# Ring items one by one and behind the maxima: a new order within the slots of an attention loop

## The reference, cut to what matters

```python
x = x + ln(attn(ln(x)))      # attn: qkv projection, 16 heads of 16, softmax, projection, z + out
x = x + ln(ffn(ln(x)))       # ffn: shared gated hidden layer of 128, and one of 8 experts for every second token
scores = einsum('bhqd,bhkd->bhqk', q, k) / 4
att = softmax(scores)
out = einsum('bhal,bhlv->bhav', att, v)
```

## Time and profile before

| | us |
|---|---|
| median of 3 runs | 984.24 (984.19 to 984.42) |
| the profiled execution | 983.9 |
| its span, first to last instruction | 982.1 |
| TensorE busy | 882.3 (90%) |
| VectorE busy | 792.7 (81%) |
| ScalarE busy | 663.7 (68%) |
| GpSimd busy | 314.5 (32%) |
| VectorE in row maxima (L1331), 1024 of them | 633.9, and 110.3 idle before them |
| ScalarE in exponentials (L873), 512 of them | 539.1, and 85.2 idle before them |

### The profile page before, as it was taken

How to read it: one execution, slowest core, us unless ns; L and a number is a source line. 1 busy time by engine, 2 the same in 40 slices (tenths; PEclk the granted TensorE clock), 3 DMA queues, 4 the chain that set the end, 5 groups by cost and what they waited for, 6 DMA issues and landing times. The chain is left out here.

```text
span 982.1 us, 14337 instructions
## 1 busy us (share of the span) xinstructions
PE 882.3 (90%) x5188; PEld 319.8 (33%) x5188; DVE 792.7 (81%) x1568; ACT 663.7 (68%) x728; POOL 314.5 (32%) x450
## 2 busy tenths in 40 slices
PE   6879999999999999999999999999989989757985
PEld 3312322222243233322332242322322313136863
DVE  4598879898979878899888879889799788265765
ACT  5128778787877787878877868788677768901110
POOL 4041010005424414139443423255243232822113
PEclk9769999999999999999999999999999989988998
DMA  5631010310320203101411022004310001240001
GB/s 143 105 45 39 16 53 16 73 41 10 90 61 13 93 12 70 38 13 55 89 61 56 12 39 59 23 7 105 91 56 14 11 13 31 85 172 23 1 1 64
DMA packets 52375, 49.08 MB, mean 50 GB/s; under 512 B 17504, under 2 KB 43696, under 8 KB 51920
## 3 DMA queue, kind: packets, MB, share of 16 engines
q1 hardware_dynamic: 51680, 46.91, 19.4%
q0 software_dynamic: 384, 1.05, 0.3%
q10 hardware_dynamic: 240, 0.20, 0.2%
HBM read 18.06 MB, written 9.17 MB: 28 GB/s over the span
## 5 line engine op out<-in xcount | busy, mean ns | idle before, releaser
L1331 DVE TENSOR_REDUCE mx<-ring 128x1 f32<-128x512 f32 x1024 | 633.9, 680 | 110.3 <-PE ring L1038 109.6
L873 ACT ACTIVATE prob<-sc,unscale 128x1024 f32<-128x1024 f32 x512 | 539.1, 1113 | 85.2 <-PE sc L1056 83.9
L1038 PE MATMUL ring<-kp,qp 48*128 48x512 f16 x1024 | 299.4, 395 | 43.5 <-DVE mx L1331 22.5
L1070 PE MATMUL obank<-prob,vaug 128*32 128x512 f32 x2048 | 276.1, 612 | 0.7 <-ACT prob L873 0.6
L1038 PEld LDWEIGHTS ring<-kp,qp 48*128 48x128 f16 x1024 | 74.1, 93 | 361.4 <-DVE mx L1331 301.3
L1056 PE MATMUL sc<-qp,kp 64*128 64x512 f16 x1024 | 167.9, 381 | 14.0 <-ACT prob L873 13.3
L644 POOL TENSOR_TENSOR parts<-qkf,parts 128x1024 f16<-128x1024 f32 x14 | 29.9, 2134 | 209.6 <-ACT parts L803 209.6
L1056 PEld LDWEIGHTS sc<-qp,kp 64*128 64x128 f16 x1024 | 50.4, 95 | 92.3 <-ACT prob L873 83.9
L631 POOL TENSOR_TENSOR hid<-hid,b 128x512 f32<-128x512 f32 x24 | 30.2, 1270 | 110.9 <-ACT hid L827 110.9
L639 POOL TENSOR_TENSOR yA<-yA,sums 128x512 f32<-128x512 f32 x15 | 19.0, 1269 | 131.1 <-DMA sums<-reciprocal_scratch 131.1
L1070 PEld LDWEIGHTS obank<-prob,vaug 128*32 128x32 f32 x2048 | 40.5, 108 | 61.5 <-issue 58.4
(11 more groups left out here) (221 smaller groups left out, 749.2 us busy)
## 6 DMA issues: line engine op xcount, KB each, us to landing
x_sb<-x SPq DMA_DIRECT2D x7, 1024.0 KB, 6.0
kp<-parts SPq DMA_DIRECT2D x48, 128.0 KB, 4.4
qp<-parts SPq DMA_DIRECT2D x93, 64.0 KB, 5.5
out<-hid SPq DMA_DIRECT2D x4, 1024.0 KB, 5.3
yA<-oT SPq DMA_DIRECT2D x124, 32.0 KB
sums<-reciprocal_scratch SPq DMA_DIRECT2D x31, 128.0 KB
x_scratch<-x SPq DMA_DIRECT2D x3, 1024.0 KB, 4.5
qp<-mp SPq DMA_DIRECT2D x128, 2.0 KB
```

Of the source, the lines that this page charges most:

```text
L873: nc.scalar.activation(prob[:, e % 2, 2 * a:2 * a + 2, :].rearrange("p g n -> p (g n)"), sbuf2[a][:, :], ACT.Exp, scale=unscale[:, 0:1]).t ...
L1038: nc.tensor.matmul(dst[:, :], qp[rows, qh, h, qt * P:(qt + 1) * P], kp[rows, h, kh * HALF:(kh + 1) * HALF], start=True, stop=True).then_in ...
L1070: ins = nc.tensor.matmul(obank[i * VW:(i + 1) * VW, :], vaug[:, b % 2, kt, c0:c0 + VW], prob[:, v % 2, i, :], start=(kt == 0), stop=(kt == ...
L1331: nc.vector.tensor_reduce(mx[:, u % 2, n:n + 1], src[:, :], AX.X, ALU.max).then_inc(rv_free, 1)
```

## The change

Within a slot TensorE now makes: maximum products 0 and 1, the value product of step e - 2, maximum products 2 and 3, the items, the scores of step e. ScalarE copies obank at the start of the slot after, ahead of the items; VectorE takes the four maxima first, then the casts, then the statistics. Items that stood in pairs get a slot each, and statistics are split and moved beside them. Slots of GpSimd's and SP's steps are moved to fit. The number of slots grows by one. No instruction is added or removed but that the statistics are taken in other portions. The diff:

```diff
--- before.py
+++ after.py
@@ -37,31 +37,32 @@
 SL = HU * NT
 NS = B * SL
 LEAD = 12
-SLOTS = NS + LEAD + 3
+SLOTS = NS + LEAD + 4
 
 
 
 QK_LEAD = (4, 5, 6, 7)
-QK_AT = (2, 2, 4, 4)
-Z_AT = ((18, 18, 20, 20), (9, 9, 17, 17))
-V_AT = (25, 25, 49, 49)
-P_AT = (19, 19, 21, 21)
-QK_NEXT_AT = (33, 33, 35, 35)
-X_AT = (41, 41, 42, 42)
-H_AT = (44, 44, 47, 47)
-U_AT = (57, 57)
-W_AT = (59, 59, 61, 61)
+QK_AT = (1, 2, 4, 5)
+Z_AT = ((17, 19, 21, 23), (9, 11, 13, 15))
+V_AT = (26, 28, 51, 53)
+P_AT = (17, 19, 22, 24)
+QK_NEXT_AT = (33, 35, 37, 39)
+X_AT = (41, 42, 43, 44)
+H_AT = (45, 46, 48, 49)
+U_AT = (57, 58)
+W_AT = (59, 60, 61, 62)
 
 MT_AT = (2, 9, 17, 25, 33, 41, 49, 57)
 
 
-Z_STATS = ((9, 10), (2, 2))
-Y_STATS = (21, 21, 25, 25)
+Z_STATS = ((9, 10), (1, 2))
+Y_STATS = (19, 22, 24, 26)
 X_STATS = (33, 35)
-F_AT = ((4, 4), (0, 1))
-
-
-D_AT = (43, 51, 14, 19)
+U_STATS = (51, 53)
+F_AT = ((4, 5), (0, 1))
+
+
+D_AT = (44, 52, 15, 21)
 
 ROWS = 16 * (1 + GH)
 
@@ -90,7 +91,7 @@
         add(1 <= w < B, W_AT, *(("w", w - 1, i) for i in range(4)))
         mt = [("mt", t // 8 - 1)] if tau in MT_AT and 0 <= t // 8 - 1 < B * HU else []
         pairs = [[("max", t, j) for j in js] if t < NS else [] for js in ((0, 1), (2, 3))]
-        at[t] = mt + fill + pairs[0] + pairs[1] if e >= 0 else pairs[0] + mt + fill + pairs[1]
+        at[t] = pairs[0] + pairs[1] + mt + fill if e >= 0 else pairs[0] + mt + fill + pairs[1]
     last = B - 1
     at[SLOTS] = ([("p", last, i) for i in range(4)]
                  + [("x", last, 0), ("x", last, 2), ("h", last, 0), ("h", last, 1), ("x", last, 1), ("x", last, 3)]
@@ -487,7 +488,7 @@
                                          mp[GH // 2 * QT * par:GH // 2 * QT * (par + 1), u % 2, j, :])\
                               .then_inc(s_mrow[u % 2], 16)
                 for u in range(B * HU):
-                    first = 8 * u + 8 + LEAD + (4 if u % HU == 0 else 1)
+                    first = 8 * u + 9 + LEAD + (4 if u % HU == 0 else 1)
                     if t == first and u < B * HU - 1:
                         result_rows(u)
                     if t == first + 3 and u < B * HU - 1:
@@ -690,14 +691,14 @@
                 if 1 <= w < B:
                     for i in slots_of(tau - 1, P_AT):
                         add("p", w - 1, i)
-                if 1 <= w < B and tau == 25:
+                if 1 <= w < B and tau == 27:
                     mean_of("y", w - 1, 0, D)
                     rstd_of("y", w - 1, 0, NT, 0)
                     pool.wait_ge(s_rstd["y"], w)
                     scaled(x1, x1, "y", 0, rstd["y"][:, 0, :], D).then_inc(s_norm["y"], 1)
                     pool.wait_ge(s_norm["y"], w)
                     nc.gpsimd.tensor_tensor(x1[:, :, :], x1[:, :, :], x_sb[:, :, :], ALU.add).then_inc(s_x1, 1)
-                if w + 1 < B and tau == 34:
+                if w + 1 < B and tau == 36:
                     second_part(w + 1, 0)
                 if 1 <= w < B and tau == 36:
                     mean_of("x", w - 1, 0, D)
@@ -713,7 +714,7 @@
                         add("h", w - 1, i)
                     for i in slots_of(tau - 1, W_AT):
                         add("w", w - 1, i)
-                if 1 <= w < B and tau == 50:
+                if 1 <= w < B and tau == 54:
                     mean_of("u", w - 1, 0, F)
                     rstd_of("u", w - 1, 0, NT, 0)
                     pool.wait_ge(s_rstd["u"], w)
@@ -857,6 +858,12 @@
             for t in range(SLOTS):
                 w, tau = divmod(t, SL)
                 e = t - LEAD
+                if e % 8 == 1 and 8 < e <= NS + 1:
+                    u = e // 8 - 1
+                    sc.wait_ge(s_av, 8 * u + 8)
+                    if u >= NH:
+                        sc.wait_ge(s_rows[u % NH], ROWS * (u // NH))
+                    nc.scalar.activation(oT[:, u % 2, :], obank[:, :], ACT.Copy).then_inc(s_oT, 1)
                 for key in RING_AT[t]:
                     if by_act(key):
                         ring_item(key)
@@ -872,14 +879,8 @@
                         sc.wait_ge(s_full, 2 * e + a + 1)
                         nc.scalar.activation(prob[:, e % 2, 2 * a:2 * a + 2, :].rearrange("p g n -> p (g n)"),
                                              sbuf2[a][:, :], ACT.Exp, scale=unscale[:, 0:1]).then_inc(s_free, 1)
-                if e % 8 == 0 and 0 < e <= NS:
-                    u = e // 8 - 1
-                    sc.wait_ge(s_av, 8 * u + 8)
-                    if u >= NH:
-                        sc.wait_ge(s_rows[u % NH], ROWS * (u // NH))
-                    nc.scalar.activation(oT[:, u % 2, :], obank[:, :], ACT.Copy).then_inc(s_oT, 1)
-                if 1 <= w < B and tau in (46, 48):
-                    i = int(tau == 48)
+                if 1 <= w < B and tau in (48, 51):
+                    i = int(tau == 51)
                     sc.wait_ge(s_added["h"], 4 * (w - 1) + 2 * i + 2)
                     tanh(2 * (w - 1) + i, 4 * i, 4)
 
@@ -1081,23 +1082,23 @@
                         elif key[0] != "max":
                             ring_item(key)
 
-                if e >= 0:
-                    items()
                 if t < NS:
                     max_products(range(0, 2))
-                if 0 <= e < NS:
-                    scores(0)
-                    scores(1)
                 if e < 0:
                     items()
                 if t in QK_LEAD:
                     i = QK_LEAD.index(t)
                     keys_or_queries(sbuf2[i // 2][:, i % 2 * HALF:(i % 2 + 1) * HALF], 2 + i // NH, i % NH)\
                         .then_inc(s_lead, 1)
+                if 0 <= e - 2 < NS:
+                    value_product(e - 2)
                 if t < NS:
                     max_products(range(2, 4))
-                if 0 <= e - 1 < NS:
-                    value_product(e - 1)
+                if e >= 0:
+                    items()
+                if 0 <= e < NS:
+                    scores(0)
+                    scores(1)
 
             last = B - 1
             row = GH * HD
@@ -1400,7 +1401,7 @@
                 w, tau = divmod(t, SL)
                 e = t - LEAD
                 for key in RING_AT[t]:
-                    if key[0] == "mt" or e < 0 and key[0] == "max" and key[2] < 2:
+                    if key[0] == "mt" or key[0] == "max" and (e >= 0 or key[2] < 2):
                         ring_item(key)
                 if w + 1 < B:
                     for i in slots_of(tau, Z_STATS[w > 0]):
@@ -1432,24 +1433,26 @@
                         if i == 1:
                             ins.then_inc(s_stats["x"], 1)
                 for u in range(B * HU - 1):
-                    if t == 8 * u + 8 + LEAD + (6 if u % HU == 0 else 3):
+                    if t == 8 * u + 9 + LEAD + (6 if u % HU == 0 else 3):
                         reciprocals(u)
-                if t == SLOTS - 5:
+                if t == SLOTS - 6:
                     ve.wait_ge(s_rows[1], ROWS * (B * HU // NH - 1))
                     half = yA[0:GH * HD, KD - 1, HALF:N]
                     nc.vector.tensor_tensor(half, half, sums[0:GH * HD, 1, :], ALU.mult).then_inc(s_div64, 1)
-                if 1 <= w < B and tau in (47, 49):
-                    n = int(tau == 49)
+                if 1 <= w < B and tau in (50, 53):
+                    n = int(tau == 53)
                     gate_first(2 * (w - 1) + n, act[:, 4 * n:4 * n + 4, :], hid[:, 4 * n:4 * n + 4, 0:F])
                     gate_second(2 * (w - 1) + n, act[:, 4 * n:4 * n + 4, :], hid[:, 4 * n:4 * n + 4, F:2 * F])
-                if 1 <= w < B and tau == 49:
-                    ve.wait_ge(s_mean["x"], w)
-                    for i in range(2):
+                if 1 <= w < B:
+                    for i in slots_of(tau, U_STATS):
+                        if i == 0:
+                            ve.wait_ge(s_mean["x"], w)
                         ve.wait_ge(s_hc, 4 * (w - 1) + 2 * i + 2)
                         ins = stats_of("u", act, 4 * i, 4, F)
-                    ins.then_inc(s_stats["u"], 1)
+                        if i == 1:
+                            ins.then_inc(s_stats["u"], 1)
                 for key in RING_AT[t]:
-                    if key[0] == "max" and (e >= 0 or key[2] >= 2):
+                    if e < 0 and key[0] == "max" and key[2] >= 2:
                         ring_item(key)
 
             last = B - 1
```

## The result

The changed kernel takes **1020.7 us** (median of 4 runs, 1019.6 to 1021.8) against 984.3 us for the kernel before on the same chip: ratio **1.0368 (95% interval 1.0350 to 1.0386)**, slower by 36.4 us. The forecast was 1003.4 with a range of 985 to 1014. The sign is right, the size is not.

A forecast was written before the change was run, and what follows sets the result against it. VectorE was taken to bound plain slots, leaving its 97.7 us of idle to change. 88.4+23.8+3.7 = 115.9, plus 18.2, with the tail plus 19.2; on 983.9 that gives 1003.1, and 0.3 for the median 1003.4, range 985 to 1014.

The forecast's parts named there:

- (d): Waits moved to GpSimd's, SP's and ScalarE's queues: 0, the first projection's scaled input having 3 us of cover.
- late inputs of the projection: Rival: residual steps ahead of GpSimd's scaling delay the projection, three boundaries at 3 to 5 us more, 1012 to 1018; chance 0.07.
- (a): VectorE's idle in the item's own slot: 1.64 long, 0.79 "w", 0.26 transposing; sum 88.4 us against 97.7.
- the prediction's own rule for a pair: TensorE time of items: a pair of 3.63 is two items of 1.73 and an entry of 0.17.
- (b): Slot behind an item: scores wait for a late exponential, VectorE idles 0.82, 0.33 or 0.16; with late value products 27.5 us.
- (c): Statistics split: slow value products of 1.93 and idles behind should vanish, some 3 us; a remaining dip costs 1.3.
- (e): Tail after the loop: the last value product comes about 1.2 later, partly hidden; plus 1.0 us (0 to 2).
- Splitting pays: Rival: (a) holds and the exponential's stall behind items is swallowed, 9.3 less in the loop, 976 with tail; chance 0.11.
- Full sharing: Rival: TensorE and VectorE share each slot fully, 60 long items give back 36 us, to 948; chance 0.03.

The follow-up runs named there:

- a_load: Changed kernel with SP's load of x for the residual issued three slots earlier (slot 8 for 11): 1006.7 us, ratio 1.0232.
- b_scale: Changed kernel with GpSimd's scaling back ahead of the residual steps (slot 14 for 15), load of x still late: 1008.6 us, ratio 1.0248.
- k_shift: Kernel before with only the change's later transfers, reciprocals and scaling; slot order, pairs and first projection item kept: 987.9 us, ratio 1.0038.
- l_p0: Changed kernel with the first two projection items in slots 19 and 20 for 17 and 19, first statistics of y later: 1010.5 us, ratio 1.0272.
- c_single: Kernel before, slot order kept, with items, statistics and gates placed one by one as in the change: 996.9 us, ratio 1.0134.
- e_after_scores: a_load with items behind the scores on TensorE and their copies behind both exponentials on ScalarE: 988.1 us, ratio 1.0035.
- i_middle: g_between_single with ScalarE taking short items between its two exponentials, and the first gates in slot 51: 978.5 us, ratio 0.9933.
- g_between_single: c_single with items between the scores and the second maximum products, ScalarE's copies behind the exponentials: 988.9 us, ratio 1.0041.
- f_between: Kernel before (pairs) with items between the scores and the second maximum products, ScalarE's copies behind the exponentials: 998.5 us, ratio 1.0136.
- j_middle_pairs: f_between with ScalarE taking the short items between its two exponentials: 981.4 us, ratio 0.9969.
- d_pairs: a_load with items and statistics in pairs again, in about the slots of the kernel before: 1010.6 us, ratio 1.0269.

## Why the prediction was right in sign and wrong in size

**The failed step is (d).** It put the waits moved to other queues at 0, "with 3 us of cover". They cost 14.0 us (1020.7 against 1006.7 in a_load, where 1003.4 was forecast), 6.8 at the first window end and 6.7 at the third, measured as the length of the maxima's group around the first projection in the two traces (33.21 for 26.41 us, 32.61 for 25.95). Two sizes in that step were wrong. The load of x was put one slot, 2.5 us, later; against the loop it is 6.0 later (2.5 and 3.5, above), because the reciprocals' transfer out now stands behind the maxima's transfers too, and the one back in behind that, which I overlooked. And it landed 9.6 us after its issue (275.33 less 265.69), where in the kernel before it takes 6.1 (the residual steps begin at 259.54). In the other kernels with the load so late it takes 7.9 (b_scale), 8.6 (k_shift) and 8.7 (l_p0); why is open. The other 6.2 of the 12.2 us is the loop itself being late: it carries TensorE along, which reached the projection not near 275.5 but near 281, and is no part of the wait. The mechanism itself was on record as the rival *late inputs of the projection*, "three boundaries at 3 to 5 us more", with a chance of 0.07; it is what happened, at two boundaries, with 6.7 to 6.8 each. What I set against it, that TensorE itself comes later, was true and not enough.

**(a) was right for the lone items, in part by luck.** 1.64 for a lone long item and 0.79 for a "w" were forecast and measured. For a transposing item 0.26 was forecast and about 0.24 measured, but the 0.52 of TensorE time behind that 0.26 does not follow from the prediction's own rule for a pair: (1.02 - 0.17)/2 + 0.17 is 0.60, c_single has gaps of 0.59, and so the forecast should have been 0.34. Behind the small transpose the forecast was too low: 1.74 + 0.13 = 1.87 for 1.71 with a hidden-layer item, 0.47 + 0.14 = 0.61 for 0.41 with a transposing one. Twenty-one items stand so.

**(b) was right for keys and queries,** 0.82 in the slot behind, with the second half of the scores held by the exponential. The lighter items were off in both directions. (For a normalizing item the prediction's terms give 0.31 and not the 0.33 that it took.) Behind a lone value item no idle is seen, where 0.16 was forecast (eight reductions in 5.16 us, of which 0.13 is the restart and 0.06 the late value product). Between items that follow one another the stall is not swallowed, as was assumed: the "x" in neighbouring slots show up to 0.45. The whole of (b), 27.5, can't be read off one run. e_after_scores takes that stall away and gives 18.6, but brings the bank waits in; taking about half of those away (i_middle without 3.1 for the gates) gives 7.2 more.

**The sum without (d):** forecast 18.2 in the loop; a_load's last group of maxima ends at 855.8 and that of the kernel before at 833.7, 22.1. The 3.9 between them are not one thing. 1.5 stands before the first group is closed (58.96 for 57.45), where the changed kernel, with the same order, has 56.96. The gates in slot 50 cost about 1.4 in each of three windows; I had listed all side work as standing beside an item, and that this work does not was in the diff. The items behind the small transpose cost up to 0.2 more each, and the missing idle behind value, projection and hidden-layer items takes some of it back. How they add up was not tried.

**(c), statistics apart, held in part:** the kernel before has value products of 1.86, 1.93 and 1.94 us in the loop's last window, two of them behind the late gates and statistics. In the changed kernel one of 1.87 is left there, at 839.58, and VectorE idles 1.02 behind it. Both statements that it would vanish were thus too strong; that a dip left over costs 1.3 was close. **(e), the tail:** 1.0 was forecast. From the last maxima to the end it was 148.4 us (982.1 less 833.7) and is 149.7 (1017.8 less 868.1), 1.3 more; in a_load, with the same order, it is 148.8, 0.4 more.

**The rivals.** *Splitting pays* fell: the exponential's stall is not swallowed. c_single shows besides that splitting by itself, with its misplaced gates, costs 12.3 us in the old order, which the prediction never asked, having costed it only inside the new one. *Full sharing* at 948 fell as well. The Trainium skill ("Perfetto Trace Analysis", Optimization Strategy) says that regimes with different bound engines may gain from being interleaved; the runs agree only so far: the same items between other neighbours, emptied earlier, give 978.5. How long ScalarE's queue keeps a ring bank is shown to cost 10 us and more of what is missing to 948 (g_between_single against i_middle, f_between against j_middle_pairs); what holds the rest is not shown.

**Still open:** how the 3.6 us of k_shift add up (two waits for the row sums, 0.94 and 1.34, are in them); why the load of x took 9.6 us to land; how much of d_pairs' 26 us is the order's, since its gates were badly placed; and what splitting costs in the old order beside the gates.

## What to carry to other kernels

Before costing a moved step at nothing, write down for each in-order queue the issue times of everything between the old and the new place, and add the landing time as measured: three small shifts (a transfer, a scaling, a consumer two slots earlier) cost 14.0 us together, and taking back any one of them gave 14.0, 12.1 or 10.2. In this loop, where one engine is fed by a ring, the place of an extra item was a choice between neighbours. Best was behind the work that a third engine needs (the scores), beside the cheaper of the two products, and with its bank emptied early; the first two without the third gave 988.9 and 998.5 us, slower than the kernel before. And side work of the bounding engine belongs in the slot where that engine idles, to the slot exactly.

## What the hardware showed that was not expected

The wait at the window end was paid twice. Windows of the changed kernel around it; columns: stretch and length in us, busy of PE, PEld, DVE, ACT and POOL with counts, granted TensorE clock, DMA share, GB/s:

```profile
275.00:281.00 6.00, 5.09 (x36) 1.18 (x33) 5.67 (x12) 4.80 (x5) 5.59 (x9) 1.00 0.56 123
281.00:286.00 5.00, 0.49 (x1) 0.50 (x2) 0.94 (x3) 0.00 (x0) 4.45 (x2) 0.73 0.03 5
286.00:290.00 4.00, 4.00 (x12) 2.31 (x13) 0.00 (x0) 0.67 (x2) 0.00 (x1) 0.50 0.32 98
```

TensorE stood idle for 4.89 us, and meanwhile the granted clock fell from 1.00 to 0.50 (from 2.4 to 1.2 GHz): the projection's eight matmuls took 3.78 us where they take 1.97 in a_load. Of the 6.8 us, 4.5 are the wait (4.89 less the 0.41 that a_load has there) and 1.8 the lower clock; 0.5 is not assigned.

The slow value products of the earlier trace rows are the same thing. Windows around the one at 790.04 in the kernel before, and around the one at 839.58 in the changed kernel:

```profile
787.00:790.00 3.00, 0.50 (x1) 0.10 (x1) 3.00 (x12) 1.35 (x2) 0.97 (x6) 0.87 0.02 3
790.00:792.00 2.00, 2.00 (x11) 0.30 (x12) 1.24 (x3) 0.00 (x0) 1.66 (x5) 0.50 0.18 66
```

```profile
836.00:838.00 2.00, 0.35 (x5) 0.05 (x1) 1.97 (x7) 0.31 (x1) 0.50 (x3) 1.00 0.22 49
839.50:841.50 2.00, 2.00 (x11) 0.28 (x12) 1.50 (x3) 1.39 (x2) 1.81 (x3) 0.55 0.00 0
```

VectorE's gates and statistics leave TensorE nearly idle (0.50 of 3.00 us, 0.35 of 2.00), the clock is then granted at 0.50 and 0.55, and the eight matmuls of a value product take 1.93 and 1.87 us instead of 1.07. So a burst of side work on VectorE costs more than its length when it starves TensorE.
